# GpSimd's stores in pairs with landing waits, and three reorderings, in a gated cross-attention and expert kernel

## The reference, cut to what matters

```
x: (8, 512, 256), context: (8, 512, 256)          # 4096 tokens of 256
x = x + tanh(g_xattn) * attention(layernorm(x), context)
    Q, K, V = projections, reshaped (16 heads, 16); per token:
    qk = Q K^T / 4 over (16, 16); softmax; values; then Wo
x = x + tanh(g_ffn) * experts(layernorm(x))
    idx = argmax(softmax(xf @ Wg + bg))             # one of 8 experts for each token
    h = gelu(xf @ W1[idx] + b1[idx]);  y = h @ W2[idx] + b2[idx]
```

## Time and profile before

| | |
|---|---|
| median of 3 runs | 296.75 us (296.5 to 297.4) |
| the profiled execution | 295.98 us |
| its span, first to last instruction | 294.1 us |
| TensorE matmul busy | 277.9 us, 94% |
| VectorE busy | 210.4 us, 72% |
| GpSimd busy | 129.4 us, 44% |
| ScalarE busy | 103.8 us, 35% |
| chain that ended last, TensorE's share | 87% |

### The profile page before, as it was taken

The page is one execution under the profiler, slowest core; times in us unless marked ns, Lnnn a source line. Parts: engine busy times, 40 slices in busy tenths (PEclk is TensorE's granted clock), DMA queues, the critical chain, the costliest instruction groups (busy, mean ns, idle before and its releaser), DMA issues.

```text
span 294.1 us, 9791 instructions
## 1 busy us (share of the span) xinstructions
PE 277.9 (94%) x3185; PEld 220.9 (75%) x3186; DVE 210.4 (72%) x613; ACT 103.8 (35%) x258; POOL 129.4 (44%) x156
## 2 busy tenths in 40 slices
PE   7999999999999999999999999899874799999994
PEld 6667777677677776776777768679763699999993
DVE  7667668786796786786877788698653666666664
ACT  2120321311303213113031131267451577777761
POOL 9613132152543624525427245413747254455455
PEclk9999999999999999999999999999999699999999
DMA  7866345476575764765746634332444244433410
GB/s 235 281 165 160 83 125 154 122 211 178 171 200 141 212 187 143 223 174 174 225 122 214 202 89 123 98 92 61 120 131 141 77 143 132 115 111 118 131 70 23
DMA packets 31240, 43.22 MB, mean 147 GB/s; under 512 B 7661, under 2 KB 18542, under 8 KB 31216
## 3 DMA queue, kind: packets, MB, share of 16 engines
q1 hardware_dynamic: 17760, 21.35, 26.7%
q10 hardware_dynamic: 10048, 12.99, 15.2%
q0 software_dynamic: 3408, 8.59, 8.2%
HBM read 24.83 MB, written 10.60 MB: 120 GB/s over the span
## 4 chain that ended last, share of the span: by engine, by line
PE 87%; DVE 3%; issue 2%; another core or an unknown queue 2%; DMA 2%; POOL 1%; ACT 1%; DVEq 0%; ACTq 0%; SPq 0%; POOLq 0%
PE ps_pr L409 18%; PE ps_qo L438 18%; PE ps_av L483 11%; PE ps_so L464 9%; PE ps_so L650 6%; PE ps_tr L650 5%; PE ps_to L669 5%; PE ps_av L669 5%; PE ps_tr L473 3%; PE ps_pr L640 3%; PE ps_to L496 2%; DMA sb_wqg<-wqg_in 2%; PE ps_pr L438 1%; PE ps_to L430 1%
## 5 line engine op out<-in xcount | busy, mean ns | idle before, releaser
L409 PE MATMUL ps_pr<-sb_wkv,sb_ct 128*128 128x512 f32 x120 | 57.7, 604 | 0.0
L723 ACT ACTIVATE sb_pe_x<-sb_pe_x 128x512 f32<-128x512 f32 x16 | 10.1, 631 | 111.5 <-DVE sb_pe_x L899 103.5
L1409 POOL DMA_INDIRECT routed_rows<-sb_xs,sb_pos_i x32 | 32.5, 1017 | 15.4 <-DVE sb_pos_i L1008 7.7
L1395 POOL TENSOR_SCALAR sb_ve<-sb_mv 128x2 f32<-128x2 f32 x16 | 3.5, 221 | 78.4 <-DVE sb_mv L858 75.9
L409 PEld LDWEIGHTS ps_pr<-sb_wkv,sb_ct 128*128 128x128 f32 x120 | 20.5, 190 | 17.7 <-issue 17.4
L483 PE MATMUL ps_av<-sb_vb,sb_at 128*32 128x128 f32 x1024 | 32.2, 274 | 1.1 <-issue 1.1
L464 PE MATMUL ps_so<-sb_kb,sb_y_q 128*32 128x128 f32 x1024 | 31.2, 273 | 0.1
L483 PEld LDWEIGHTS ps_av<-sb_vb,sb_at 128*32 128x32 f32 x1024 | 27.2, 110 | 5.0 <-issue 4.9
L438 PE MATMUL ps_qo<-sb_wog,sb_ot 128*128 128x264 f32 x120 | 29.6, 388 | 0.0
L438 PEld LDWEIGHTS ps_qo<-sb_wog,sb_ot 128*128 128x128 f32 x120 | 22.5, 190 | 9.2 <-issue 6.4
L438 PE MATMUL ps_qo<-sb_wqg_c,sb_xt 128*128 128x264 f32 x120 | 29.3, 387 | 0.0
(11 more groups left out here) (158 smaller groups left out, 493.9 us busy)
## 6 DMA issues: line engine op xcount, KB each, us to landing
sb_x<-x_in ACTq DMA_DIRECT2D x16, 256.0 KB, 3.5
sb_kb<-sb_y_k SPq DMA_DIRECT2D x124, 32.0 KB
sb_vb<-sb_y_v SPq DMA_DIRECT2D x120, 32.0 KB
sb_ct<-ctx_in ACTq DMA_DIRECT2D x14, 256.0 KB, 3.2
sb_xt<-xt_in_ ACTq DMA_DIRECT2D x14, 256.0 KB, 4.3
sb_xb<-routed_rows SPq DMA_DIRECT2D x25, 134.0 KB
sb_w_all<-w_in_ SPq DMA_DIRECT2D x4, 514.0 KB
sb_w<-w_in SPq DMA_DIRECT2D x4, 512.0 KB
```

Source lines behind the costliest of these rows:

```text
L409: last = pe.matmul(pr[:, s * 512:(s + 1) * 512], lhsT=ct[i][:, kc, s, :], rhs=wkv[:, :, kc, :], start=(kc == 0), stop=(kc == KC - 1))
L723: act.activation(pe_x[:], pe_x[:], ACT.Exp, scale=float(H) ** -0.5).then_inc(exp_done, 1)
L1409: pool.indirect_dma_start(rows, bass.IndirectOffsetOnAxis(ap=row_numbers(batch)[:, c:c + 1], axis=0), rows_of(j)[:, s, :], None).then_inc( ...
```

## The change

Four parts.

1. GpSimd. The four routes of the last batch come together behind the store of block 3, in two pairs, and GpSimd waits after each pair until it has landed. The stores are in pairs of an even and an odd block: behind the odd one GpSimd waits until the even one has landed, up to block 35 (not in the pair of 2 and 3, where the routes' waits stand).
2. VectorE at the end of the first stage: `place_2` and `place_3` of batch 6 come ahead of the residual of pair 15.
3. TensorE: slots 2 to 15 are written out, and the matmul that spreads `lap` comes behind slot 14 instead of slot 13; slots 16 to 31 are a loop of two turns of eight, 32 to 39 are written out.
4. VectorE at the end: block 38's `prepare` comes in slot 36, behind that of block 36, and writes to a buffer of its own in the free tile `y_q`; it has no wait for an earlier sum. The waits on `yl_done` follow the new order.

```diff
+YL_ORDER = (0, 2, 1)
...
-            def slots_4(first, turns):
-
-                with pe.Fori(0, turns) as turn:
-                    for k in range(first, first + W1_RING):
-                        expert_slot(W1_RING * turn + k, k % W1_RING, turn)
-
-            for b in range(2, 6):
+            for b in range(2, EARLY):
...
-            slots_4(6, 2)
-            pe.wait_ge(lap_done, 1)
-            pe.matmul(lap_ps, lhsT=ones[:], rhs=lap_d[:], start=True, stop=True).then_inc(lap_spread, 1)
-            slots_4(14, 5)
-            for b in range(34, blocks + 1):
-                expert_slot(b, b % RING, b // RING)
+                if b == RING + 6:
+                    pe.wait_ge(lap_done, 1)
+                    pe.matmul(lap_ps, lhsT=ones[:], rhs=lap_d[:], start=True, stop=True).then_inc(lap_spread, 1)
+            block_slots(pe, expert_slot, 1)
...
+            def yl(b):
+                return y_q[:].rearrange("p a b h -> p (a b h)")[:, 0:D] if b == blocks - 1 else yo[b % 2][:]
...
-                dve.wait_ge(yf_done, b - 1)
+                if b < blocks - 1:
+                    dve.wait_ge(yf_done, b - 1)
                 dve.wait_ge(stored[j], 16 * (b // OUT))
-                dve.scalar_tensor_tensor(yo[i][:], b2_sb[:, bass.ds(ex, 1), :].rearrange("p a d -> p (a d)"), tg[:, 1:2],
+                dve.scalar_tensor_tensor(yl(b), b2_sb[:, bass.ds(ex, 1), :].rearrange("p a d -> p (a d)"), tg[:, 1:2],
...
-                dve.wait_ge(yl_done, b - (blocks - AHEAD) + 1)
+                dve.wait_ge(yl_done, YL_ORDER.index(b - (blocks - AHEAD)) + 1)
...
                 place_1(m)
+                place_2(m)
+                place_3(m)
                 residual(n + 1, (n + 1) % 4)
-                place_2(m)
                 stats_1(n + 1, (n + 1) % 4)
-                place_3(m)
                 stats_2(n + 1, (n + 1) % 4)
...
-                if known and blocks - AHEAD <= b < blocks:
+                if known and blocks - AHEAD <= b < blocks - 1:
                     prepare(b)
+                if known and b == blocks - AHEAD:
+                    prepare(blocks - 1)
...
             for b in range(EARLY):
                 store(b, b % RING, b // RING)
-                if b in (2, 3):
-                    route_nth(last_batch, 2 * b - 4)
-                    route_nth(last_batch, 2 * b - 3)
-            block_slots(pool, store, 0)
+                if b == 3:
+                    for i in range(4):
+                        route_nth(last_batch, i)
+                        if i % 2 == 1:
+                            pool.wait_ge(routed, 32 * pairs - 16 * (3 - i))
+                elif b % 2 == 1:
+                    pool.wait_ge(stored[(b - 1) % OUT], 16 * ((b - 1) // OUT + 1))
+            def store_in_twos(b, q, turn):
+                store(b, q, turn)
+                if isinstance(b, int) and b >= blocks - 3:
+                    return
+                if q % 2 == 1 and isinstance(b, int):
+                    pool.wait_ge(stored[q - 1], 16 * (turn + 1))
+                elif q % 2 == 1:
+                    wait_apart(pool, stored[q - 1], 16 * (turn + 1), passed_pool)
+
+            block_slots(pool, store_in_twos, 0)
```

More of the change, by code:

```diff
@@ L1137, in finish @@
                 dve.scalar_tensor_tensor(yf[j], yo[i][:], tg[:, 1:2], xb[q][:, 0:D], ALU.mult, ALU.add).then_inc(yf_done, 1)
+            def yl(b):
+                return y_q[:].rearrange("p a b h -> p (a b h)")[:, 0:D] if b == blocks - 1 else yo[b % 2][:]
             def prepare(b):
-                i, j = b % 2, b % OUT
+                j = b % OUT
                 x_b = xb[b % RING]
                 ex = dve.value_load(tab[0:1, 1, b:b + 1], min_val=0, max_val=E - 1)
-                dve.wait_ge(yf_done, b - 1)
+                if b < blocks - 1:
+                    dve.wait_ge(yf_done, b - 1)
                 dve.wait_ge(stored[j], 16 * (b // OUT))
-                dve.scalar_tensor_tensor(yo[i][:], b2_sb[:, bass.ds(ex, 1), :].rearrange("p a d -> p (a d)"), tg[:, 1:2],
+                dve.scalar_tensor_tensor(yl(b), b2_sb[:, bass.ds(ex, 1), :].rearrange("p a d -> p (a d)"), tg[:, 1:2],
                                          x_b[:, 0:D], ALU.mult, ALU.add).then_inc(yl_done, 1)
@@ L1156, in finish_ahead @@
                     dve.wait_ge(y_done, b + nth + 1)
-                    last = dve.scalar_tensor_tensor(yf[j][:, first:end], src, tg[:, 1:2], yo[i][:, first:end], ALU.mult, ALU.add)
+                    last = dve.scalar_tensor_tensor(yf[j][:, first:end], src, tg[:, 1:2], yl(b)[:, first:end], ALU.mult, ALU.add)
                 last.then_inc(yf_done, 1)
```

## The result

The changed kernel takes 292.35 us (median of 6 runs, 290.89 to 293.13), the kernel before beside it 296.84 us (296.07 to 297.4). The ratio is 0.9847, with a 95% interval of 0.9825 to 0.9868: faster by 1.5%. The forecast was 286.0. The profiled execution took 291.02 us with a span of 289.2; it is the second fastest of the six and has the highest granted clock, 0.996 where the others have 0.991 to 0.995. The span is 4.9 us shorter than before, where the sum said 10.75.

The account below looks back on a forecast made before the run. TensorE was taken to bound the kernel, losing 12.70 us before block 11, mostly to signals held behind GpSimd's DMA trains. Terms -1.6, -1.35, -6.1, -2.0 and +0.3 sum to -10.75: 295.98 - 10.75 + 0.77 = 286.0 us, range 283.6 to 297.0.

Parts of the forecast that it names:

- Landing waits of the stores: GpSimd's waits behind store pairs: nothing from block 16 on, 0.1 us or so per next store in a backlog.
- The tail: End of the kernel: the last bias order puts the last store later, +0.3 us (between -0.3 and +0.7).
- The holds: TensorE's signals held behind GpSimd's trains: -1.35 us of 2.35 at blocks 6 to 8, -6.1 of 6.58 at 9 to 10.
- Row numbers ahead: Row-number cast before the last residual: routes 1.75 us earlier, TensorE's wait of 1.33 ends, -1.6 (0 to -1.6).
- Half clock: Matmuls at 1.2 GHz behind TensorE's idle time, blocks 10 to 11: the clock should hold, -2.0 us (0 or -2.0).
- Unrolling: TensorE's slots written out in the expert stage: no matmul changes, 0 us.
- the rival of the branch: TensorE's branch at its first turn's end causes the 4.13 us stop; unrolling gains it, 290.6 us, chance 0.05.
- Last bias ahead: VectorE's bias of block 38 before block 36's sum: delays store 37, +0.3 us (-0.3 to +0.7).
- the wait does not cut trains: Backlogged stores still go 1.3 us apart, a train of eight from 222.9 holds TensorE: 296.2 us, chance 0.14.
- The stores pile up: More than eight stores due behind the routes from 222.9, each costing 1.3 us: eleven give 300.1, chance 0.14.
- One train stays in part: Late signals behind the first train or a shorter second one, clock still falls: 289 to 293, centre 291, chance 0.20.

Follow-up runs that it names:

- e3: The changed kernel without landing waits of the stores from block 16 on: 295.74 us, ratio 0.996 to the kernel before.
- e10: The changed kernel with a 768-number GpSimd fill replacing each store landing wait, routes' waits kept, on a chip with stops: 291.8 us against 296.22.
- e12: The changed kernel with GpSimd pauses replacing the landing waits of both stores and routes: 290.81 us against 296.22 for the kernel before.
- e7: The changed kernel with block 38's bias in its old place, on the chip without stops: 290.01 us against 283.5 for the kernel before.
- e8: The changed kernel with TensorE's old loops, on the chip without stops: 291.61 us against 283.5 for the kernel before.
- e1: The changed kernel with GpSimd's old order, without landing waits; the other parts stay: 297.34 us against 296.75 for the kernel before.
- e2: The kernel before with only GpSimd's part of the change: 291.98, 291.99, 294.87 and 297.07 us; ratio 0.9873 without the last.
- e15: The kernel before with three groups of three stores and one of four issued together: 309.19 us in a single run, against 296.48.
- e13: The changed kernel with a pause of two 384-number fills behind every second GpSimd transfer and no landing wait: 288.19 us against 296.48.
- e9: The changed kernel itself, run again on a chip with stops: 292.22 us against 296.22 for the kernel before.
- e16: The changed kernel itself, run again beside the version in twos with pauses: 292.32 us against 296.48 for the kernel before.
- e14: The kernel before with GpSimd's transfers in twos, a two-fill pause between and no landing wait: 288.7 us against 296.48.
- e4: The changed kernel without any landing waits of the stores, the routes' waits kept: 297.95 us against 296.75, ratio 1.0031.
- e17: The changed kernel in twos without landing waits, the pause cut to one fill of 384 numbers: 294.68 us against 296.51 for the kernel before.
- e18: The changed kernel in twos without landing waits, the pause cut to one fill of 64 numbers: 296.46 us against 296.51 for the kernel before.
- e6: The kernel before with stores of blocks 16 to 23 in twos, 24 to 31 in fours, chip without stops: 283.57 us in one run, against 283.5.
- e5: The changed kernel with a 768-number GpSimd fill replacing each store landing wait, on the chip without stops: 282.62 us against 283.5.
- e11: The kernel before with stores of blocks 16 to 23 in twos, 24 to 31 in fours, chip with stops: 303.8 us in one run.

## Why the prediction was wrong, step by step

The gain was 4.9 us of span instead of 10.75. The step that failed is "Landing waits of the stores": "the first of a pair has landed 2.63 after its start", "In a backlog it delays the next store by 0.1 or so", and "From block 16 on the wait ends before the next result (1.98 a block, 3.96 a pair): nothing". With it failed the tail's **+0.3**. The 2.63 was read from one store, the last of the kernel before, when hardly anything else ran. In the change a store took 2.3 to 4.3 us to land, 3.3 in the mean, and 0.40 more passed to the next issue. So a pair takes 3.72 where two stores without a wait take 2.57: the wait delays the next store by 1.15, not by 0.1. GpSimd comes out of the routes about five blocks late (store 4 at 225.52, by the prediction 222.9), gains 0.24 a pair on TensorE instead of 1.39, and is late to the end. An estimate from these numbers: with 2.63 and 0.40 a pair would take 3.03, and the five blocks would have been made up in 11 of the 15 pairs. Why the landings are longer in the middle of the kernel, no run shows.

Two terms make up the difference of 5.85:

- **The tail**, +0.3 in the sum, measured +3.3: 3.0 of the 5.85. The prediction computed the backlog for 222.9 on and asked only whether it makes trains, not when it ends. That the waits make the tail is shown: without those from block 16 on it is 1.64 (e3), and with a pause in their place 1.34 and 1.35 (e10, e12). On the second chip the same waits gave a tail of 8.3 (e7) and a stop of 2.6 (e8), where they had nothing to win.
- **The holds**, -1.35 and -6.1 in the sum. Counted slot by slot as the prediction did, they came to about -0.8 and -4.5. Block 11 was forecast for 222.7 by the sum (222.5 in the text) and came at 224.98, and 0.5 more was lost on the way to the end (56.99 us from there to TensorE's end, before 56.47). Sign and place were right, and e1 and e2 show that it is GpSimd's order that does it. But twos with landing waits don't end the hold fully: 0.20, 0.81, 1.13 and 0.42 idle are left. Both times a group stands ahead of them that is longer than two: 207.06 to 211.00 (two routes, two stores) and 213.93 to 217.81 (two stores, two routes). The prediction had the first of these, and took it that the wait behind it would free the signals; e15's threes show why it must hold, and e13, in which these groups are cut, has none of these waits. e12 has the first of them and a stop of 3.31.

The two are not independent. In the six traces with landing waits (the change, e2, e7, e8, e9, e16) the last store starts between 285.25 and 287.82, while TensorE ends anywhere from 277.15 to 285.93. So a TensorE that lost less would most likely have ended earlier and left a longer tail; that is argued from six traces and was not tried by itself.

Point by point otherwise:

- **Row numbers ahead**, -1.6: the cast was forecast for 202.1 and came at 202.21, TensorE's wait of 1.33 is gone. Right in the profile. In the time it is worth less: e1 shows nothing, since a later stop takes it back, and between e14 and e13, without the long stops, lie 1.3 us of span of the profiled executions and 0.5 of the medians, for all three reorderings together.
- **Half clock**, -2.0: right in the profiled execution, whose clock line is full, and there luck has a part. In the profiles of the same kernel on two other chips the clock fell (e9 and e16, granted clock 0.988 and 0.989; before 0.988). It also came back with most of the longer stops (e1, e3, e4, e12, e17, e18: matmuls of 1.70 to 2.08).
- **Unrolling**, 0: e1 has the unrolled slots and the old stops; e14 has the old loops, on a chip with stops, and none where the first turn ends; nor have e6 and e8. No effect is shown, and the rival of the branch has fallen. The Trainium skill (Runtime: NRT & Kernel Launch, Instruction fetch mechanics) speaks of a stall for a taken branch out of the loaded pages; no run here shows one at these loops.
- **Last bias ahead**: not measured. On the chip of e7 the stores' tail hides it.
- **Rivals**: "the wait does not cut trains" has fallen by e4 (no waits at the stores: 1.0031 of before, where the change, in the comparison of the result, is at 0.9847). "The stores pile up" named the right place and the wrong harm: they pile up, but as a tail and not as a train. "One train stays in part" (291) is nearest in number, and half of it is right: the first group of four did hold.
- **Why landing waits are dear**: the prediction cited the Trainium skill (DMA: Bandwidth & Descriptors, Anatomy of one DMA) for about 2.0 us fixed, most of it completion, and set it aside because slots of 1.98 cover it. The trace agrees with that size for the transfer at 281.27 (2.29), but not for the others, which took up to 4.3. It was the objection to take seriously: cover exists only for an engine that is on time.

What e13 shows is that the forecast's gain was there: 288.19 us against 292.32 of the change, with the trains cut by fixed pauses. From 286.0 it is 2.2 away, of which 1.0 is the late load and about 1.0 the tail of 2.55 (the sum had 1.26 + 0.3), for GpSimd with its pauses still does not wait for a result in the last pairs.

**Still open.** Why trains hold TensorE's signals on four of the experiments' chips and not on the one of e5 to e8; the runs show that they do, by length and by break, and not through what. Whether the changed kernel and e13 themselves do on the second chip what e7, e8 and e5 make likely (slower by some 3%, and no slower). From what break on nobody is held: 0.60 us is too short, 0.93 nearly enough, 1.1 enough in e13. Why a store takes 2.3 us to land at one time and 4.3 at another.

## What to carry to other kernels

A wait that is covered in the steady state is not covered for an engine that is behind: work out how late the engine is when it gets there and how fast it can catch up, before the wait is costed at nothing, and take the length of a transfer from rows in which as much runs beside it as will in the place of the wait. When several engines stand still at once though their matmul is recorded as over, look at what GpSimd issues at that time, and change the spacing of its transfers (pairs with 1.1 us of other work between them did it here, with 0.9 almost) rather than wait for them to land. And measure on more than one chip: the same edit was 1.1 to 1.5% faster on some, and two near copies of it were 3% slower on another.

## What the runs showed of the hardware

- Indirect DMAs that GpSimd issues 1.28 us apart (0.98 issuing, 0.30 between) delay the moment at which the other engines hear of TensorE's finished matmuls on four of the five chips, and TensorE by that: by up to 0.15 us for two, 0.9 for three, 2.2 and 2.6 for four and five, 3.1 and 3.8 for six (e11, e15). With pairs, breaks of 0.34 and 0.60 us did not end it (e18, e17), one of 0.93 did but for one wait of 0.92 (e12, e10), and 1.1 did (e13).
- On the other chip, that of e5 to e8, twenty of them in a row delayed nothing (e6), and the kernel before took 283.5 us instead of 296.2 to 296.8.
- Behind the longer stops the clock fell to its lower level, 1.2 GHz, but not always with the first matmuls: layer 2 took 2.07 us instead of 1.03 right behind stops of 2.59, 3.48 and 4.17 (e17, e18), while behind 3.31 and 3.56 (e12, e18) it took 1.13 and the layer 1 that follows it 1.70 and 1.92 instead of 1.06. Behind one of 2.23 (e10) no matmul took longer than 1.16.
- A store of 128 rows that was waited for took 2.3 to 4.3 us from its start to its landing in one trace of the change, and 0.40 more to the next issue, where a queued one starts 0.30 behind the one before.
